# Attention on one core: value products for two head pairs at a time, and output products kept turned until the end of a batch

## The chip, the cores and the metric

The kernel runs on one core of one Trainium2 chip. The metric is the device time of one execution in microseconds (us), lower is better; a kernel's figure is the median of its runs. All data are float32 unless a row says bf16.

## The reference, cut to what matters

The program is one transformer-like block over x of shape (2, 1024, 128): a recurrent mixer, a feed-forward layer with one of 32 experts for each token, a multi-level (hierarchical) attention, and the same feed-forward layer again. The change is in the attention alone:

```python
qkv = x @ w_qkv.T                      # 16 heads of 64, x is layer-normed
q, k, v = split(qkv)
for level in range(...):               # level 0 and five coarser levels
    # coarser q, k are means of neighbours, coarser v are sums of neighbours
    A = exp(S - S.max(-1))             # S in blocks of 16, q of a block with k of the block before
    Ysum += A @ v;  Asum += A.sum(-1)
out = Ysum / (Asum + 1e-8)
out = out @ w_out.T + b_out            # summed over the 16 heads
x = x + out
```

## The kernel before, in words

The five engines run five instruction streams written by hand; semaphores alone join them. PE is TensorE, DVE VectorE, ACT ScalarE, POOL GpSimd, SP the engine that issues DMAs.

The attention (functions `b_pe`, `b_act`, `b_dve`, `b_pool_engine`, `b_sp`) works on 16 units: 2 batches of 1024 tokens times 8 pairs of heads (a pair is 128 columns). The tokens of the level 0 (1024) and the coarser ones (512 places) make 12 tiles of 128. FINE is the level 0, ROUGH the coarser levels. `b_pe` is a software pipeline of iterations n = 0 to 16; iteration n begins with the four products `project(n+1, ...)` (L1730), and then has, in this order: ROUGH scores of unit n (L1763, L1769), `project_last(n+1)` (L1737), `values(n+1)` (L1748: 12 products, the loaded operand a tile of tokens, the moving one the 128 columns of value weights), extra work of other layers (turning of x in iterations 2 and 3, routing of the next layer in 11 to 14), `weighted(n, FINE)` (L1800), `project_out(n-1)` (L1821: 8 products, the loaded operand 128 tokens of the unit's normalised output, the moving one 128 columns of output weights, so that tokens lie on partitions), `weighted(n, ROUGH)`, FINE scores of unit n+1, and `add_weights(n)` (L1810). Iteration 15 has no projections; 16 is the end.

What the other engines do in iteration n, in order:
- ACT: `copy_y(n-1)`, the four drains of `project` (L1916), the exponential of unit n FINE (L1931), the drains of `project_last` and of the values (L1920 to L1924), the exponential ROUGH (L1935).
- DVE: `soften(n, FINE)` (L2024, L2025, L2030: maximum, subtraction, transposition), `divide(n-1)` (L2034 to L2041: reciprocals of the sums), `soften(n, ROUGH)`, `gather_out(n-1, 0)` and `(n-1, 1)` (L2050, which waits for `project_out`), `coarsen(n+1)` (L2068, L2071).
- POOL: two multiplications that normalise unit n-1 (L2200), then `merge(n)` (L2137, five additions, after the exponential ROUGH of n), for which `add_weights(n)` waits. In between now and then: `add_bias` (L2165) and, for the second batch, the coarser sums and `pack(1)` (L2146).

The products of `project` with j = 0, 1, of `project_last`, `values` and `project_out` pass through two PSUM banks in turn; the list `filled` fixes the order, and `bank_free` waits for the reader two fillings back.

## Time and profile before

| | |
|---|---|
| median of 3 runs (lowest to highest) | 561.32 us (560.02 to 562.15) |
| the profiled execution | 560.87 us, span 559.1 us |
| mean granted PE clock | 0.969 |
| PE busy | 506.0 us, 91% |
| DVE busy | 425.8 us, 76% |
| ACT busy | 291.5 us, 52% |
| POOL busy | 250.6 us, 45% |

The attention takes the stretch from about 217 to 465 us. A float32 product shows as two MATMUL records and two weight loads. The rows quoted below are from stretches of this; their columns are start in us, length in us, engine, line, operation, and in brackets the idle time before with what ended it.

### The profile page before, as it was taken

To read this page: it belongs to the slowest core of one execution; us is meant where nothing else is said; L and a number is where in the kernel's file an instruction comes from. 1 tells how busy PE (TensorE), PEld (TensorE's weight loads), DVE (VectorE), ACT (ScalarE), POOL (GpSimd) and SP (SyncE) were. 2 spreads that over 40 slices of the span, in tenths; PEclk is the share of its full clock that TensorE was granted. 3 is DMA by queue.
4 is the path that set the end of the run, shared out by engine and by line. 5 is a ranking of instruction groups with operands and counts; after the bars stand their busy time and mean duration, and the time that the engine had idled before them with its cause. 6 is when DMAs were issued, how large, how long until landed. Compare 5 with 4: busy or idle time off the path is not lost.

```text
span 559.1 us, 16575 instructions
## 1 busy us (share of the span) xinstructions
PE 506.0 (91%) x6408; PEld 307.2 (55%) x6408; DVE 425.8 (76%) x979; ACT 291.5 (52%) x624; POOL 250.6 (45%) x294
## 2 busy tenths in 40 slices
PE   6989888888989998999999999999999967989991
PEld 3323232356544544777767777777777755644540
DVE  3396958988747766878899888899878988847762
ACT  3644254254458864666545555546644523448870
POOL 3556677655524454252244443233333335533542
PEclk9999899998999998999999999999999987899997
DMA  6899820000269962100000000000000000169964
GB/s 182 319 426 270 94 25 0 2 0 20 66 194 277 273 211 67 31 3 21 21 21 22 22 21 22 22 21 22 22 20 9 7 2 9 40 184 277 277 215 137
DMA packets 45325, 54.09 MB, mean 97 GB/s; under 512 B 10880, under 2 KB 36416, under 8 KB 44224
## 3 DMA queue, kind: packets, MB, share of 16 engines
q1 hardware_dynamic: 42688, 47.78, 29.6%
q0 software_dynamic: 2560, 5.26, 2.7%
q8 instruction: 51, 0.84, 0.6%
q14 instruction: 26, 0.21, 0.1%
HBM read 43.55 MB, written 9.48 MB: 95 GB/s over the span
## 4 chain that ended last, share of the span: by engine, by line
PE 63%; DVE 22%; issue 6%; DMA 3%; ACT 3%; POOL 2%; SPq 0%; DVEq 0%; POOLq 0%; ACTq 0%
PE psum L1249 9%; PE psum L1748 7%; PE psum L1730 7%; PE psum L1821 5%; PE psum L1800 5%; PE psum L1268 4%; PE psum L1769 3%; PE psum L1256 3%; DVE arena L761 3%; POOL sorted_x L1467 2%; DVE arena L755 2%; PE psum L277 2%; PE psum L278 2%; PE psum L1007 1%; DVE arena L2030 1%
## 5 line engine op out<-in xcount | busy, mean ns | idle before, releaser
L2200 POOL TENSOR_TENSOR arena<-arena 128x512 f32<-128x512 f32 x32 | 40.9, 1302 | 110.6 <-issue 103.9
L1495 POOL DMA_INDIRECT y_tok<-arena,to x48 | 46.6, 971 | 63.3 <-ACT arena L1318 62.1
L1916 ACT ACTIVATE arena<-psum 128x512 f32<-128x512 f32 x64 | 38.1, 597 | 47.4 <-PE psum L1730 44.4
L1730 PE MATMUL psum<-arena 128*128 128x512 f32 x128 | 59.2, 605 | 0.7 <-ACT arena L1899 0.7
L1249 PE MATMUL psum<-experts,arena 128*32 x96 | 50.2, 604 | 1.1 <-ACT arena L1308 1.1
L1249 PE MATMUL psum<-arena 128*32 128x512 f32 x288 | 50.9, 605 | 0.0
L661 POOL TENSOR_TENSOR arena<-arena 128x512 f32<-128x512 f32 x32 | 37.2, 1179 | 27.9 <-DVE arena L761 17.5
L1748 PE MATMUL psum<-arena 128*128 128x128 f32 x384 | 47.5, 278 | 0.8 <-ACT arena L1921 0.8
L1748 PEld LDWEIGHTS psum<-arena 128*128 128x128 f32 x384 | 45.2, 192 | 1.8 <-ACT arena L1921 1.8
L2137 POOL TENSOR_TENSOR arena<-arena 128x256 f32<-128x256 f32 (+4 forms) x75 | 33.6, 447 | 25.9 <-ACT arena L1935 18.9
L1730 PEld LDWEIGHTS psum<-arena 128*128 128x128 f32 x128 | 22.9, 189 | 35.4 <-issue 33.8
L1332 ACT ACTIVATE arena<-experts 128x768 f32 x48 | 40.1, 839 | 1.7 <-issue 1.4
L1467 POOL DMA_INDIRECT sorted_x<-arena,row x32 | 31.0, 969 | 20.3 <-DVE row L1099 11.8
L1391 DVE COPY arena<-psum 128x256 f32<-128x256 f32 x48 | 20.4, 425 | 25.4 <-PE psum L1256 25.0
L761 DVE TENSOR_TENSOR_SCAN arena<-psum,arena 128x512 f32<-128x512 f32 x32 | 39.1, 1269 | 0.0
L1800 PE MATMUL psum<-arena 64*64 64x64 f32 (+2 forms) x1728 | 36.9, 224 | 2.2 <-ACT arena L1931 1.4
L2050 DVE TENSOR_TENSOR x_tok<-x_tok,psum 128x512 f32<-128x512 f32 x30 | 20.6, 687 | 22.7 <-PE psum L1821 22.5
L1924 ACT ACTIVATE arena<-psum 128x512 f32<-128x512 f32 x48 | 28.7, 597 | 17.2 <-PE psum L1748 17.2
L1268 PEld LDWEIGHTS psum<-experts,arena 128*32 128x32 f32 x192 | 20.8, 110 | 30.2 <-issue 29.8
L1800 PEld LDWEIGHTS psum<-arena 64*64 64x64 f32 x1728 | 33.1, 138 | 6.3 <-ACT arena L1931 1.5
L1821 PE MATMUL psum<-arena 128*128 128x128 f32 x256 | 34.0, 286 | 2.7 <-POOL arena L2200 2.7
L755 DVE TENSOR_TENSOR arena<-arena,psum 128x512 f32<-128x512 f32 x32 | 19.9, 685 | 20.9 <-PE psum L293 20.7
(240 smaller groups left out, 1195.2 us busy)
## 6 DMA issues: line engine op xcount, KB each, us to landing
arena<-in_experts SPq DMA_DIRECT2D x48, 384.0 KB, 4.4
experts<-in_experts SPq DMA_DIRECT2D x8, 1536.0 KB, 17.3
arena<-sorted_x SPq DMA_DIRECT2D x48, 64.5 KB, 3.7
sorted_x<-zeros SPq DMA_DIRECT2D x2, 1536.0 KB, 14.3
arena<-in_w_qkv SPq DMA_DIRECT2D x16, 192.0 KB, 2.8
arena<-y_tok SPq DMA_DIRECT2D x8, 256.0 KB, 3.1
x_tok<-in_x SPq DMA_DIRECT2D x4, 256.0 KB, 4.6
arena<-in_w_out SPq DMA_DIRECT2D x16, 64.0 KB, 1.9
```

Of the source, the lines that this page charges most:

```text
L761: dve.tensor_tensor_scan(a_state[:, m, 1:CHUNK + 1], DECAYS[:, :], a_kv[m % HALF], a_state[:, m, 0:1], ALU.mult, ALU.add).then_inc(s["stat ...
L1249: mm = pe.matmul(bank[2 + s % 2][rows, :], f_gxt[s % 2][:, rows], weights, start=True, stop=True)
L1268: mm = pe.matmul(bank[6 + s % 2][SLOT_ROWS * j:SLOT_ROWS * j + SLOT_ROWS, 0:C], f_sht[s % 2][:, rows], weights, start=(half == 0), stop=(h ...
L1332: act.activation(f_w_act[s % 5], experts[:, bass.ds(expert_at[s], WROW)], ACT.Copy).then_inc(t["w_act"], 1)
L1467: pool.indirect_dma_start(out=sorted_x[k], out_offset=bass.IndirectOffsetOnAxis(ap=f_row[:, i:i + 1], axis=0), in_=row_of(k, i), in_offset ...
L1495: pool.indirect_dma_start(out=y_tok, out_offset=bass.IndirectOffsetOnAxis(ap=f_to[:, s:s + 1], axis=0), in_=f_gy[(s + 4) % 8], in_offset=N ...
L1730: pe.matmul(ring("in", n, j)[:, :], b_w[n % 2][:, which * P:which * P + P], x, start=True, stop=True)\
L1748: mm = pe.matmul(ring("in", n, 5 + i // 4)[:, i % 4 * P:i % 4 * P + P], x, b_w[n % 2][:, 2 * P:3 * P], start=True, stop=True)
L1800: mm = pe.matmul(place(Y[r][out]), b_v[n % 2][rows, i, out], e[rows, head, i - part.start, cols], start=(i == 0), stop=last_place(r, i, cols))
L1821: mm = pe.matmul(ring("out", n, i // 4)[:, i % 4 * C:i % 4 * C + C], b_yn[:, i * P:i * P + P], b_wo[n % 2], start=(n < LAST - 1 or n < LAS ...
L1916: act.activation((b_q, b_k)[which][:, part * CHUNK:part * CHUNK + CHUNK], src, ACT.Copy, scale=(D_B ** -0.5, 1.0)[which]).then_inc(h["drai ...
L2200: pool.tensor_tensor(b_yn[:, part], b_y[:, part], b_rec[:, part], ALU.mult).then_inc(h["normed"], 1)
```

## The change

Values: the loads of value weights are split off from those of q and k weights. `values(n)` runs for even n alone and makes the values of units n and n+1: the loaded token tile is the same, the moving operand is 256 columns. Iterations with odd n have this work, those with even n have none; the first stands ahead of iteration 0. Value drains on ACT are six in the one iteration (before: three in each). Outputs: for 13 units `project_out` loads the output weights and moves 512 tokens past them, twice, so that channels lie on partitions; the sums of a batch are kept so in `b_acc`. For the last unit of batch 0 and the last but one of batch 1 (`TURNED_BACK`), the sums are turned back by products of `b_acc` tiles with the identity into the bank, into which these units' outputs then go in the old way. The bias joins the first sum on DVE in place of POOL's `add_bias`. The normalised output replaces `b_y` in place. ACT packs only what of `b_odd` is used.

```diff
-            sp.dma_start(b_w[n % 2].rearrange("p (n c) -> p n c", c=P), w["w_qkv"][n % PAIRS]).then_inc(w_in[n % 2], 16)
+            sp.dma_start(b_w[n % 2].rearrange("p (n c) -> p n c", c=P), w["w_qkv"][n % PAIRS][:, 0:2]).then_inc(w_in[n % 2], 16)
+
+        def value_weights_in(sp, n):
+            two = w["w_qkv"][n % PAIRS:n % PAIRS + 2, :, 2:3].rearrange("u c n d -> c (n u) d")
+            sp.dma_start(b_wv.rearrange("p (u d) -> p u d", d=P), two).then_inc(wv_in, 16)
...
+        TURNED_BACK = (PAIRS - 1, LAST - 1)
...
             def values(n):
                 b = n // PAIRS
+                pe.wait_ge(wv_in, 16 * (n // 2) + 16)
                 for i in range(TILES_B):
-                    if i % 4 == 0:
-                        bank_free("in", n, 5 + i // 4)
+                    if i % 2 == 0:
+                        bank_free("in", n, 5 + i // 2)
...
-                    mm = pe.matmul(ring("in", n, 5 + i // 4)[:, i % 4 * P:i % 4 * P + P], x, b_w[n % 2][:, 2 * P:3 * P],
+                    mm = pe.matmul(ring("in", n, 5 + i // 2)[:, i % 2 * 2 * P:i % 2 * 2 * P + 2 * P], x, b_wv,
                                    start=True, stop=True)
...
+            def turn_sums(n, j):
+                pe.wait_ge(h["acc"], 2 * (n - 1) + j + 1)
+                for i in range(4):
+                    pe.matmul(ring("out", n, j)[:, i * C:i * C + C], b_acc[:, j * CHUNK + i * P:j * CHUNK + i * P + P], ident,
+                              start=(i == 0), stop=False)
+
             def project_out(n):
                 pe.wait_ge(wo_in[n % 2], 16 * (n // 2) + 16)
...
+                for j in range(2):
+                    out = ring("out", n, j)
+                    if n < LAST:
+                        bank_free("out", n, j)
+                    if n in TURNED_BACK:
+                        turn_sums(n, j)
+                    pe.wait_ge(h["normed"], 2 * n + j + 1)
+                    y = y_of(n)[:, j * CHUNK:j * CHUNK + CHUNK]
+                    if n in TURNED_BACK or n == LAST:
+                        for i in range(4):
+                            mm = pe.matmul(out[:, i * C:i * C + C], y[:, i * P:i * P + P], b_wo[n % 2], start=False,
+                                           stop=(n != LAST - 1 and i == 3))
+                    else:
+                        mm = pe.matmul(out, b_wo[n % 2], y, start=True, stop=True)
+                    mm.then_inc(h["o"], 1)
...
-                if new:
+                if new and n % 2 == 1:
                     values(n + 1)
...
             def gather_out(n, j):
-                dve.wait_ge(h["biased"], n // PAIRS + 1)
                 dve.wait_ge(h["o"], 2 * n + j + 1)
                 at = n // PAIRS * SEQ + j * CHUNK
-                part = slice(at, at + CHUNK)
-                dve.tensor_tensor(x_tok[:, part], x_tok[:, part], ring("out", n, j)[:, :], ALU.add)\
-                   .then_inc(h["acc"], 1)
+                part, acc = slice(at, at + CHUNK), b_acc[:, j * CHUNK:j * CHUNK + CHUNK]
+                if n % PAIRS == 0:
+                    dve.wait_ge(bias_in, 16)
+                    i = dve.tensor_scalar(acc, ring("out", n, j)[:, :], b_bias, None, ALU.add)
+                elif n % PAIRS == PAIRS - 1:
+                    i = dve.tensor_tensor(x_tok[:, part], x_tok[:, part], ring("out", n, j)[:, :], ALU.add)
+                else:
+                    i = dve.tensor_tensor(acc, acc, ring("out", n, j)[:, :], ALU.add)
+                i.then_inc(h["acc"], 1)
```

PE's stream before, from the start of iteration 3 to the output products of iteration 4 (left out: iteration 3's smaller products). Each iteration has its own `values`, L1748, between L1737 and L1800.

```order
L1730 MATMUL psum<-arena 128x512 x4
L1763 MATMUL psum<-attend_bf 128x256 x2
L1769 MATMUL psum<-arena 64x64 x16
L1737 MATMUL psum<-arena 128x128 x2
L1748 MATMUL psum<-arena 128x128 x12
L1800 MATMUL psum<-arena 64x64 x32
L1821 MATMUL psum<-arena 128x128 x8
```

The same engine now, in an iteration with even n. Nothing stands between L1757 (`project_last`) and L1821 (`weighted`), and L1856 is the output product.

```order
L1750 MATMUL psum<-arena 128x512 x4
L1784 MATMUL psum<-attend_bf 128x256 x2
L1790 MATMUL psum<-arena 64x64 x16
L1757 MATMUL psum<-arena 128x128 x2
L1821 MATMUL psum<-arena 64x64 x32
L1856 MATMUL psum<-arena 128x512 x2
```

And now in an iteration with odd n, where the twelve products L1769 have 256 columns.

```order
L1784 MATMUL psum<-attend_bf 128x256 x2
L1790 MATMUL psum<-arena 64x64 x16
L1757 MATMUL psum<-arena 128x128 x2
L1769 MATMUL psum<-arena 128x256 x12
L1821 MATMUL psum<-arena 64x64 x32
L1856 MATMUL psum<-arena 128x512 x2
```

So the value products of two iterations have moved together ahead of the FINE `weighted` of the odd one.

## Rows read from the trace of the kernel before

**Rows 1.** Stretch, length; busy PE, PEld, DVE, ACT, POOL; PE clock, DMA: iterations 0,2,4,7,10,12,14.

```profile
226.86:239.92 13.06, 12.56 (x255) 8.60 (x253) 9.58 (x35) 7.83 (x15) 5.68 (x8) 1.00 0.12 32
254.12:268.79 14.67, 14.67 (x276) 10.87 (x273) 12.16 (x22) 9.26 (x19) 4.69 (x7) 1.00 0.07 20
283.46:298.70 15.24, 14.62 (x272) 10.58 (x269) 14.23 (x28) 7.23 (x14) 5.97 (x10) 1.00 0.07 20
327.12:341.33 14.21, 14.21 (x273) 10.45 (x269) 12.29 (x22) 7.35 (x14) 4.70 (x7) 1.00 0.08 22
370.24:384.98 14.74, 14.58 (x273) 10.59 (x269) 13.65 (x32) 8.86 (x18) 5.90 (x8) 1.00 0.08 20
399.62:415.60 15.98, 15.73 (x285) 11.82 (x281) 12.28 (x23) 8.00 (x16) 4.69 (x7) 1.00 0.07 18
431.71:448.03 16.32, 15.01 (x274) 10.72 (x270) 15.73 (x28) 7.92 (x16) 5.91 (x9) 1.00 0.02 6
```

**Rows 2.** Timeline of PE in iteration 7.

```profile
327.12 3.70 PE L1730 MATMUL psum<-arena 128*128 128x512 f32 x8
...
331.59 0.71 PE L1737 MATMUL psum<-arena 128*128 128x128 f32 x4
332.14 2.90 PE L1748 MATMUL psum<-arena 128*128 128x128 f32 x24
334.97 1.16 PE L1800 MATMUL psum<-arena 64*64 64x64 f32 x64
336.06 2.05 PE L1821 MATMUL psum<-arena 128*128 128x128 f32 x16
338.04 1.08 PE L1800 MATMUL psum<-arena 64*64 64x64 f32 x44
```

**Rows 3.** Product lines by themselves: duration of one in ns, minimum/median/maximum.

```profile
L1748 PEld LDWEIGHTS psum<-arena x384: 186/192/192, 224.0 to 440.3; 128*128 128x128 f32 x192
L1748 PE MATMUL psum<-arena x384: 275/275/377, 224.1 to 440.4; 128*128 128x128 f32 x192
L1730 PE MATMUL psum<-arena x128: 592/592/697, 217.7 to 434.8; 128*128 128x512 f32 x128
```

**Rows 4.** Timeline of DVE in iteration 7 and the start of 8.

```profile
326.86 1.21 DVE L2024 TENSOR_REDUCE arena<-psum 128x16 f32<-128x1024 f32 x1
...
335.17 0.71 DVE L2030 STREAM_TRANSPOSE arena<-arena 128x512 f32<-128x512 f32 x1
...
340.94 1.21 DVE L2024 TENSOR_REDUCE arena<-psum 128x16 f32<-128x1024 f32 x1
```

**Rows 5.** Timeline of ACT in iteration 7: the exponentials and the last value drain.

```profile
331.35 1.05 ACT L1931 ACTIVATE arena<-arena 128x1024 f32<-128x1024 f32 x1
...
335.08 0.60 ACT L1924 ACTIVATE arena<-psum 128x512 f32<-128x512 f32 x1 [0.35 <-PE psum L1748]
335.92 0.81 ACT L1935 ACTIVATE arena<-arena 128x256 f32<-128x256 f32 x3 [0.24 <-DVE arena L2030]
```

**Rows 6.** Timeline of POOL: end of iteration 6, then iteration 7.

```profile
325.63 1.37 POOL L2146 COPY arena<-arena 128x128 f32<-128x128 f32 x6
333.23 2.54 POOL L2200 TENSOR_TENSOR arena<-arena 128x512 f32<-128x512 f32 x2 [6.23 <-issue]
336.81 2.48 POOL L2137 TENSOR_TENSOR arena<-arena 128x256 f32<-128x256 f32 x5 [1.04 <-ACT arena L1935]
```

**Rows 7.** Timeline of DVE: `soften` FINE of iterations 4 and 10.

```profile
285.00 1.21 DVE L2024 TENSOR_REDUCE arena<-psum 128x16 f32<-128x1024 f32 x1
...
371.27 1.22 DVE L2024 TENSOR_REDUCE arena<-psum 128x16 f32<-128x1024 f32 x1
```

**Rows 8.** Timelines of DVE and POOL around `add_bias` in iteration 3.

```profile
281.49 2.20 DVE L2068 TENSOR_TENSOR arena<-arena 128x128 f32<-128x128 f32 x1
...
281.16 2.38 POOL L2165 TENSOR_TENSOR x_tok<-x_tok,arena 128x1024 f32<-128x1024 f32 x1
```

**Rows 9.** Timeline of PE: output products of unit 15.

```profile
461.74 1.13 PE L1821 MATMUL psum<-arena 128*128 128x128 f32 x8 [2.30 <-POOL arena L2200]
```

More of the change, by code:

```diff
@@ L1545, in f_sp @@
             if k == 0:
-                for n in range(2):
-                    attention_weights_in(sp, n)
+                attention_weights_in(sp, 0)
+                value_weights_in(sp, 0)
+                attention_weights_in(sp, 1)
             else:
@@ L1562, in hybrid_block @@
         b_rstd = [b_rstd_all[:, CT * c:CT * c + CT] for c in range(STEPS)]
-        b_w = [carve(3 * P) for _ in range(2)]
+        b_w, b_wv = [carve(2 * P) for _ in range(2)], carve(2 * P)
         assert F_ROWS_AT <= B_EARLY_AT and used[0] <= F_LOOP_AT
@@ L1606, in hybrid_block @@
             if n + 1 < UNITS:
-                filled += [("in", n + 1, j) for j in range(IN) if j not in IN_Y]
+                filled += [("in", n + 1, j) for j in range(fills(n + 1)) if j not in IN_Y]
             filled += AMONG.get(n, [])
@@ L1685, in merged_columns, with y_of @@
                     (fine[64:128, :, 31:512:32], rough[64:128, :, 3, 48:64])]
+        def y_of(n):
+            return b_y if n < LAST else b_q[:, 0:SEQ]
         def last_place(r, i, cols):
@@ L1705, in bank_free @@
                     after(pe, h["y_out"], n - 1)
-                    after(pe, h["drained"], IN * (n - 1) + IN_Y[-1] + 1)
+                    after(pe, h["drained"], filled_by(n - 1) + IN_Y[-1] + 1 if n else 0)
                     return
@@ L1711, in bank_free @@
                     if kind == "in":
[L1712 removed]
+                        pe.wait_ge(h["drained"], filled_by(n) + j + 1)
                     elif kind == "turn":
@@ L1754, in scores @@
                 rough = part == ROUGH
-                pe.wait_ge(h["drained"], IN * n + (5 if rough else 4))
+                pe.wait_ge(h["drained"], filled_by(n) + (5 if rough else 4))
                 if rough:
@@ L1789, in weighted @@
                 pe.wait_ge(h["expd"], 2 * n + rough + 1)
-                pe.wait_ge(h["drained"], IN * n + (8 if rough else 7))
+                pe.wait_ge(h["drained"], filled_by(n // 2 * 2) + (11 if rough else 9))
                 if not rough:
@@ L1799, in weighted @@
                             for cols, place in places(r, i):
-                                mm = pe.matmul(place(Y[r][out]), b_v[n % 2][rows, i, out], e[rows, head, i - part.start, cols],
+                                mm = pe.matmul(place(Y[r][out]), values_of(n)[rows, i, out], e[rows, head, i - part.start, cols],
                                                start=(i == 0), stop=last_place(r, i, cols))
@@ L1902, in pack @@
             def pack(b):
-                for level in range(1, LEVELS + 1):
+                for level in range(3, LEVELS + 1):
                     act.wait_ge(h["pooled"], pooled_up_to(level, b))
@@ L1948, in copy_y @@
                 act.wait_ge(h["weighed"], 2 * n + 2)
-                after(act, h["normed"], 2 * n)
-                act.activation(b_y, psum[:, 4 * 512:6 * 512], ACT.Copy).then_inc(h["y_out"], 1)
+                if n < LAST:
+                    after(act, h["o"], 2 * n)
+                act.activation(y_of(n), psum[:, 4 * 512:6 * 512], ACT.Copy).then_inc(h["y_out"], 1)
             act.activation(b_warm, constant("half")[:, 0:1], ACT.Exp)
@@ L1957, in b_act @@
             pack(0)
-            for j in range(4, IN):
+            for j in range(4, fills(0)):
                 drain(0, j)
@@ L1974, in b_act @@
                 if new:
-                    for j in range(4, IN):
+                    for j in range(4, fills(n + 1)):
                         drain(n + 1, j)
@@ L2058, in coarsen @@
                 for which, a in enumerate((b_q, b_k)):
-                    dve.wait_ge(h["drained"], IN * n + 2 * which + 2)
+                    dve.wait_ge(h["drained"], filled_by(n) + 2 * which + 2)
                     if which == 0:
@@ L2078, in b_dve @@
                 dve.wait_ge(returned[j], 16 * (RUNS // 4 - 1))
-            for a in (b_odd, b_even):
-                chain(dve.memset(rough_columns(a)[:, :, 3, 0, 48:64], 0.0))
+            for a, deep in ((b_odd, 0), (b_even, 3)):
+                chain(dve.memset(rough_columns(a)[:, :, deep, 0, 48:64], 0.0))
             pool_first(0)
@@ L2198, in b_pool_engine @@
                     pool.wait_ge(h["divided"], 2 * n + j + 1)
-                    after(pool, h["o"], 2 * (n - 1) + j + 1)
-                    pool.tensor_tensor(b_yn[:, part], b_y[:, part], b_rec[:, part], ALU.mult).then_inc(h["normed"], 1)
+                    pool.tensor_tensor(y_of(n)[:, part], y_of(n)[:, part], b_rec[j], ALU.mult).then_inc(h["normed"], 1)
                 if n + 1 < LAST:
```

83 lines of the change are left out of this document (37 added, 46 removed).

## The prediction

> **What bounds the kernel now.** I read first the busy time by stretch, cut at the starts of the iterations [rows 1]. The reader is to see three things: the typical iteration (7) takes 14.21 us and PE is busy in all of it; DVE is busy 12.29 of the 14.21 us, so it is close behind; and iterations 4, 10 and 14 are longer while PE is not full in them (14.62 of 15.24, 14.58 of 14.74, 15.01 of 16.32), so there something else decides. The granted clock is 1.00 in all. Second, PE's timeline of iteration 7 [rows 2], from start to start: projections and ROUGH scores 4.47 us, `project_last` 0.55, values 2.83, `weighted` FINE 1.09, output products 1.98, and from 338.04 to the next start at 341.33 another 3.29. Third, the other engines in the same iteration [rows 4 to 6], for what PE would wait for if it came earlier.
>
> Call s the start of `soften` FINE on DVE. Here s is 326.86, 0.26 us before the iteration begins (327.12), and in iteration 8 340.94, 0.39 before. From s runs a chain through all engines: DVE's three pieces of work (soften FINE, divide, soften ROUGH) end at 335.17 + 0.71 = s + 9.02 [rows 4]; ACT's ROUGH exponential runs from 335.92 to 336.73, POOL's merge from 336.81 to 339.29 [rows 5, 6]; then PE's `add_weights` and the next iteration. How long this chain is when it alone decides is read from the iterations in which PE waited: iteration 10 has s = 371.27 and ends at 384.98, iteration 4 has s = 285.00 and ends at 298.70 [rows 1, 7]. That is 13.71 and 13.70 us from s to the end. So an iteration cannot be shorter than 13.7 us from its s, however little PE has to do, and with s 0.3 before its start that is 13.4 us. The typical iteration is only 0.8 us longer than that. This is the number on which the forecast rests.
>
> **The change part by part.**
>
> Value products, on PE. Of one pair of units, 48 products' records with 128 columns become 24 with 256. Start to start, a record of 128 columns takes (2.90 - 0.275) / 23 = 0.114 us, one of 512 (3.70 - 0.592) / 7 = 0.444 [rows 2, 3]: nearly in proportion to columns. One of 256 is in none of the rows; it lies between half of 0.444 = 0.222 and twice 0.114 = 0.228. I take 0.223, so 24 of them take 5.35 us where two sections took 5.66: 0.3 us less in a pair, 2.5 in all eight.
>
> Output products. 16 records of 128 columns (1.98 us) become 4 of 512; half the length of `project`'s eight is 1.82. So 0.16 less in each of 13 units, 2.1 in all. The sums turned back cost 16 records for each of two units: 16 x 0.114 = 1.8 us each. In iteration 8 they stand ahead of a wait and are mostly in its shadow (0.2 us on the path). After the output products of unit 14, PE waits 2.30 us for POOL until it can begin those of unit 15 at 461.74 [rows 9]; 1.8 us more fits in this. If that cover were gone it would cost 1.8 us.
>
> The moved values are what counts. An iteration with odd n now has 14.21 - 2.83 + 5.35 - 0.16 = 16.57 us of work on PE, 2.35 more than before; nothing on the other engines comes up to that. Seven of them (1 to 13): +16.45. In two of these (9 and 13) DVE starts late because of work for the next layer, and ACT's exponential, which stands ahead of the value drains, delays the second group of values by part of a drain; estimate 0.2 each, +0.4.
>
> An iteration with even n has only 14.21 - 2.83 - 0.16 = 11.22 us of work on PE. It does not take 11.22, for the chain needs 13.4. Followed in order, from the iteration's start: PE wants `weighted` FINE at 5.02; ACT's exponential of it ends at 332.40, or 5.28 after the start [rows 5], 0.4 us of waiting. It wants the output products at 6.6; POOL's first multiplication, 333.23 + 1.27, ends at 7.4 and the second at 8.65 [rows 6], 1.3 us of waiting in two parts, and the products end at 9.75. It wants `weighted` ROUGH then; the exponential ends at 9.61. It would be ready for `add_weights` at 12.1; merge ends at 12.17. With 0.2 for the release and 0.97 for the work: 13.4, the same from PE's side as from the chain. DVE cannot be further ahead at the start, for `gather_out` waits for the output products, which in the long iteration ahead stand behind the values; from their end DVE needs what it needs now, and s stays 0.3 before the start.
>
> The even iterations one by one, against their length now [rows 1]. Iteration 2: 14.67 to 13.4, -1.3. Iteration 4: 15.24 to 13.4, -1.85; 1.0 of this is `add_bias` that is gone, for DVE's addition next to it took 2.20 us instead of about 0.28 [rows 8]. Iterations 6 and 8: 14.21 to 13.6 (POOL's sums for the second batch lie late in the one, the sums turned back are in the other), -0.6 each. Iteration 10 is bound by the chain now and has its statistics on DVE ahead of s still: 0. Iteration 12 has 1.77 us of routing on PE, s at about -0.25: 15.98 to 13.7, -2.3. Iteration 14: bound by other engines now, 0. Iteration 0: the values of units 0 and 1 stand ahead of it, which moves its start by 2.5 us; after that its ROUGH scores, at 3.63 + 1.1, set off 2.2 of DVE, 0.85 of ACT, 2.5 of POOL and 1.2 of release and `add_weights`, 11.45 us in place of 13.06: +0.9. Together -5.75. Also `pack(1)` on POOL, 1.37 us, stands behind merge at the end of iteration 6 [rows 6], and PE waits for it before iteration 7; merge now ends only 1.2 us before the end: +0.4.
>
> Costs of nothing: the six value drains take 0.60 us each [rows 5] for every 0.89 us of filling, as now. `b_y` in place: `project_out(n-1)` stands ahead of `weighted(n, ROUGH)` on PE, and the copy waits for the latter anyway. The bias on DVE replaces an addition of the same size. The extra DMA on SP stands behind value products that are done two iterations before its data are wanted. ACT's shorter pack is in time in which ACT is idle (7.35 busy of 14.21 [rows 1]).
>
> Sum: 16.45 + 0.4 + 0.4 - 5.75 = +11.5 us. Against the profiled execution (560.87, of it 559.1 span; nothing ahead of the attention or behind it changes) this is 572.4. The profiled run lies 0.45 below the median of the three runs, 561.32; I put the forecast at 572.5.
>
> **The weight loads.** A value product of 128 columns has a load of 192 ns beside it, and the products follow each other every 114 ns [rows 3], so loads lie beside products and beside each other. If a section's pace were set by its loads, a product with 256 columns would take as long as one with 128.
>
> The Trainium skill, page "TensorE: Matmul & The Clock Gate", section "Back-to-back issue gap", says that in a stream of loads and products the spacing is set by both, with about 81 ns at 128 columns and 131 at 512. By that ratio of 1.6 the 512-column form would be far cheaper for each column; this trace has 0.444 to 0.114, a ratio of 3.9, for float32, so I go by the trace.
>
> **The rivals.**
> - The even iterations do shrink to PE's own work (faster). For this merge would have to end at 10 in place of 12.2, that is, s would have to lie 2.5 us before the start in place of 0.3; from 2.2 us on the loss begins to vanish. Then the even iterations save 3.0 (4.0 in iteration 4), 22 in all, against 16.9 + 0.4 for the odd ones and 1.8 for the sums turned back: about -3.5, 557 us. Against it stand iterations 4 and 10, where the chain held at 13.7 us twice. Chance 0.07.
> - The loads set the pace of the products (faster). The values of a pair then take 2.83 in place of 5.66. The odd iterations stay near 14.1, the even ones at 13.4: 16.45 falls to about -1, which gives 555 us. Against it: 114 ns under a load of 192. Chance 0.04.
> - No gain and no loss: the even iterations give back about as much as the odd ones take, for instance with the merge on POOL quicker in the gaps. It needs 1.6 us less in each even iteration. Chance 0.05.
> - The odd iterations also wait for ACT (slower still). Each group of two tiles is filled in 0.89 us and must be drained before the next but one; if the drain, now with a strided read, and the release take 0.3 us more than 0.60, six groups wait 0.15 each, 0.9 us in an iteration, and if the clock falls in the gaps of the even ones another 1 us each. Together +6 to +14 on the 11.5: about 580. Chance 0.12.
> - As worked out, with its own range of 568 to 577, as the chain is known to 0.3 us in eight iterations and the odd ones to 0.4: chance 0.72.
>
> **How the numbers follow.** The likeliest gives 572.5. To leave out no more than two in ten, the range takes in the lower part of the slower rival and some way towards no change: 564 to 580. Less than 0.5% (2.8 us) is about what a measurement of this kernel can't tell from no change. Faster by more: 0.07 x most of it and 0.04, 0.10. Within: 0.06. Slower: 0.84.
>
> **What would show it.** In the profile after, iterations with odd n should be 16.6 us with PE full, and those with even n 13.4 with PE busy about 11.2, waiting at `weighted` FINE for ACT, at the output product for POOL's multiplication, and at `add_weights` for POOL's merge. DVE, busy the same in both, should idle before `gather_out` for some 4 us in the odd ones and hardly in the even ones. Products of 256 columns should start every 0.22 us. The prediction is wrong if even iterations are below 13 us, if `values` takes less than 5.2 us, or if the waits stand in the odd ones.

## The result, and the profile after

The changed kernel takes 575.95 us (median of 4 runs, 573.62 to 576.79) against 561.63 us before (4 runs, 560.02 to 562.15): a ratio of 1.0247, 95% interval 1.0211 to 1.0282. The profiled execution is one of 575.73 us with a span of 573.9 us, 14.8 more than the span before, and a mean granted clock of 0.971 (before 0.969). PE is busy 509.0 us, 3.0 more than before, in a span 14.8 longer: its share has gone from 91% to 89%. The work has hardly changed, the waiting has.

I cut the trace at the starts of the iterations as before. Busy time by stretch of the changed kernel, iterations 0, 2, 4, 5, 7, 10, 12 and 14 (columns as in [rows 1]):

```profile
228.80:240.11 11.31, 9.83 (x229) 5.89 (x229) 8.03 (x25) 6.16 (x12) 4.59 (x7) 1.00 0.09 25
256.89:270.50 13.61, 12.40 (x240) 6.93 (x236) 12.85 (x22) 7.58 (x16) 4.70 (x7) 1.00 0.06 17
287.82:301.44 13.62, 12.05 (x237) 6.55 (x233) 12.86 (x22) 5.57 (x11) 5.69 (x9) 1.00 0.06 17
301.44:318.22 16.78, 16.78 (x261) 10.58 (x257) 11.78 (x22) 9.05 (x17) 6.38 (x12) 1.00 0.08 22
332.31:349.06 16.75, 16.75 (x256) 10.55 (x256) 11.49 (x21) 9.04 (x17) 4.51 (x7) 1.00 0.08 22
379.85:395.86 16.01, 13.32 (x237) 7.17 (x233) 14.11 (x32) 7.16 (x15) 5.81 (x8) 0.89 0.05 14
413.12:426.75 13.63, 13.26 (x248) 7.89 (x245) 12.87 (x25) 6.44 (x13) 4.70 (x7) 1.00 0.07 18
444.88:461.22 16.34, 12.41 (x238) 6.68 (x234) 15.79 (x28) 6.21 (x13) 5.75 (x9) 1.00 0.02 6
```

The reader is to see the alternation: with odd n (5, 7) 16.8 us and PE busy in all of it; with even n (2, 4, 12) 13.6 us, in which PE is not full and DVE is busy 12.9. Iteration 10 stands out with 16.01 us and a clock of 0.89.

PE's timeline in iteration 7, which answers to [rows 2]:

```profile
337.31 5.53 PE L1769 MATMUL psum<-arena 128*128 128x256 f32 x24
342.77 1.16 PE L1821 MATMUL psum<-arena 64*64 64x64 f32 x64
343.86 1.99 PE L1856 MATMUL psum<-arena 128*128 128x512 f32 x4
345.78 1.08 PE L1821 MATMUL psum<-arena 64*64 64x64 f32 x44
```

The values take 342.77 - 337.31 = 5.46 us (before 2.83), the output products 345.78 - 343.86 = 1.92 (before 1.98). And the same engine in iteration 4, an even one:

```profile
293.16 1.16 PE L1821 MATMUL psum<-arena 64*64 64x64 f32 x64
295.33 2.32 PE L1856 MATMUL psum<-arena 128*128 128x512 f32 x4 [1.01 <-POOL arena L2227]
297.65 1.08 PE L1821 MATMUL psum<-arena 64*64 64x64 f32 x44
...
300.42 1.09 PE L1831 MATMUL psum<-arena 64*64 64x512 f32 x8 [0.27 <-POOL arena L2177]
301.44 1.13 PE L1750 MATMUL psum<-arena 128*128 128x512 f32 x2
```

PE waits twice for POOL: 1.01 us for the normalisation (L2227), and again before `add_weights` (L1831) for the merge (L2177). The groups of the attention (212 to 480 us) say the same for all iterations; behind the second bar stand the idle times and what ended them:

```profile
L1769 PE MATMUL psum<-arena 128*128 128x256 f32 x192 | 44.8, 387 | 0.3 <-ACT arena L1953 0.2
L1821 PE MATMUL psum<-arena 64*64 64x64 f32 (+2 forms) x1728 | 37.8, 227 | 5.2 <-ACT arena L1964 2.9 <-ACT arena L1968 1.9
L1856 PE MATMUL psum<-arena 128*128 128x512 f32 x52 | 27.6, 638 | 7.2 <-POOL arena L2227 6.6
L1831 PE MATMUL psum<-arena 64*64 64x512 f32 x120 | 15.9, 602 | 1.5 <-POOL arena L2177 1.4
```

The value products (L1769), now in odd iterations alone, wait 0.3 us in all, in iterations 9 and 13.

**The books.** All figures are differences to before in us. The stretch ahead of the attention -0.77 (the first `project` starts at 216.91, before at 217.68; over the ten kernels of this text it starts at 216.9 to 220.7, so I take it for chance, which is not shown). The values of the second unit ahead of iteration 0, together with iteration 0: +0.96 (11.89 in place of 9.18, then 11.31 in place of 13.06). Odd iterations 1 to 13: +17.45. Even iterations 2 to 12: -4.47. Iteration 14: +0.02. From there to the second layer's scatter: -0.45. The second layer: +2.0, which is not the change's (below). Sum 14.7.

### The profile page after: what moved, and what is told of

It is laid out like the page before. It is cut to its first block, busy times and chain, and to the rows that moved or that the text cites. A ratio compares the mean times of both kernels' runs of the same rounds, so it can differ in the third digit from the quotient of the medians.

```text
span 573.9 us, 15923 instructions
## 1 busy us (share of the span) xinstructions
PE 509.0 (89%) x6092; PEld 281.6 (49%) x6092; DVE 425.5 (74%) x979; ACT 290.7 (51%) x618; POOL 243.1 (42%) x292
## 4 chain that ended last, share of the span: by engine, by line
PE 53%; DVE 28%; issue 7%; POOL 4%; DMA 3%; ACT 3%; SPq 0%; DVEq 0%; POOLq 0%; ACTq 0%
PE psum L1249 8%; PE psum L1769 7%; PE psum L1750 6%; PE psum L1268 4%; PE psum L1856 3%; PE psum L1256 3%; PE psum L1821 3%; DVE arena L2064 3%; DVE arena L2059 2%; DVE arena L761 2%; POOL sorted_x L1467 2%; DVE arena L2058 2%; PE psum L277 2%; DVE arena L755 2%; PE psum L278 2%
## 5 line engine op out<-in xcount | busy, mean ns | idle before, releaser
L2227 POOL TENSOR_TENSOR arena<-arena 128x512 f32<-128x512 f32 x32 | 37.6, 1195 | 112.1 <-DVE arena L2076 112.1
L1750 PE MATMUL psum<-arena 128*128 128x512 f32 x128 | 59.1, 605 | 1.0 <-ACT arena L1931 0.7
L2177 POOL TENSOR_TENSOR arena<-arena 128x256 f32<-128x256 f32 (+4 forms) x75 | 34.3, 458 | 45.5 <-ACT arena L1968 37.6
L661 POOL TENSOR_TENSOR arena<-arena 128x512 f32<-128x512 f32 x32 | 37.2, 1182 | 27.8 <-DVE arena L761 17.5
L1769 PE MATMUL psum<-arena 128*128 128x256 f32 x192 | 44.8, 387 | 0.3 <-ACT arena L1953 0.2
L1821 PEld LDWEIGHTS psum<-arena 64*64 64x64 f32 x1728 | 34.0, 140 | 19.7 <-ACT arena L1968 7.8
L1821 PE MATMUL psum<-arena 64*64 64x64 f32 (+2 forms) x1728 | 37.8, 227 | 5.2 <-ACT arena L1964 2.9
L1750 PEld LDWEIGHTS psum<-arena 128*128 128x128 f32 x128 | 23.0, 189 | 35.9 <-issue 34.4
L1769 PEld LDWEIGHTS psum<-arena 128*128 128x128 f32 x192 | 33.0, 189 | 9.8 <-ACT arena L1957 3.6
L755 DVE TENSOR_TENSOR arena<-arena,psum 128x512 f32<-128x512 f32 x32 | 19.8, 683 | 20.9 <-PE psum L293 20.7
L2090 DVE TENSOR_TENSOR arena<-arena,psum 128x512 f32<-128x512 f32 x22 | 14.8, 678 | 25.9 <-PE psum L1856 25.9
L1856 PE MATMUL psum<-arena 128*128 128x512 f32 x52 | 27.6, 638 | 7.2 <-POOL arena L2227 6.6
```

What stands on the lines that cost most here:

```text
L1750: pe.matmul(ring("in", n, j)[:, :], b_w[n % 2][:, which * P:which * P + P], x, start=True, stop=True)\
L1769: mm = pe.matmul(ring("in", n, 5 + i // 2)[:, i % 2 * 2 * P:i % 2 * 2 * P + 2 * P], x, b_wv, start=True, stop=True)
L1821: mm = pe.matmul(place(Y[r][out]), values_of(n)[rows, i, out], e[rows, head, i - part.start, cols], start=(i == 0), stop=last_place(r, i, ...
L1856: mm = pe.matmul(out, b_wo[n % 2], y, start=True, stop=True)
L2227: pool.tensor_tensor(y_of(n)[:, part], y_of(n)[:, part], b_rec[j], ALU.mult).then_inc(h["normed"], 1)
```

## Lengths of the iterations in all kernels

Call s, as in the prediction, the start of `soften` FINE on DVE; the chain is the time from s to the end of the iteration, and the lead is how far s lies ahead of the iteration's start.

Each experiment below has one thing to be read from its trace before its whole time: how long the iterations are. Lengths in us, from the starts of the `project` products in PE's timeline of each profiled execution; "0 to 13" is the sum of iterations 0 to 13, "ahead" the time from the first `project` to iteration 0.

| kernel | ahead | 1 | 2 | 4 | 5 | 7 | 8 | 9 | 10 | 11 | 12 | 0 to 13 |
|---|---|---|---|---|---|---|---|---|---|---|---|---|
| before | 9.18 | 14.20 | 14.67 | 15.24 | 14.21 | 14.21 | 14.21 | 14.70 | 14.74 | 14.64 | 15.98 | 204.85 |
| changed | 11.89 | 16.78 | 13.61 | 13.62 | 16.78 | 16.75 | 13.62 | 17.17 | 16.01 | 17.26 | 13.63 | 216.08 |
| values per unit | 9.18 | 14.15 | 14.60 | 14.15 | 14.15 | 14.15 | 16.00 | 15.01 | 14.46 | 14.58 | 15.91 | 204.95 |
| paired values only | 11.89 | 16.84 | 13.57 | 15.49 | 16.85 | 16.81 | 13.57 | 16.84 | 15.96 | 17.32 | 13.70 | 217.88 |
| no values | 11.90 | 12.93 | 13.00 | 12.98 | 12.98 | 12.68 | 13.48 | 14.90 | 15.15 | 13.70 | 13.13 | 189.02 |
| statistics later | 11.89 | 16.78 | 13.63 | 13.59 | 16.79 | 16.75 | 13.61 | 17.18 | 13.68 | 17.26 | 13.74 | 213.84 |
| values spread | 11.89 | 14.09 | 14.86 | 14.64 | 14.10 | 14.10 | 16.18 | 14.96 | 15.49 | 14.53 | 16.03 | 207.66 |
| spread, statistics later | 11.89 | 14.09 | 14.86 | 14.64 | 14.09 | 14.10 | 16.18 | 14.96 | 14.64 | 15.54 | 16.03 | 207.83 |
| merge cut short | 11.89 | 16.78 | 13.06 | 12.99 | 16.78 | 16.79 | 13.47 | 17.17 | 14.52 | 17.26 | 13.13 | 211.79 |
| wait alone | 9.18 | 14.20 | 14.67 | 15.45 | 14.21 | 14.21 | 14.21 | 15.02 | 14.96 | 14.65 | 15.97 | 205.46 |

Iterations repeat to a few hundredths from kernel to kernel where nothing in them is changed (1, 9 and 11 of the changed kernel, of the one with late statistics and of the one with the merge cut short). The rest of a program does not: from iteration 14's start to the end of the span it is 127.4 us before and 128.1 to 134.3 in the others, though behind the attention the instructions are the same. So small effects are read from iterations.

## The experiments

**The values unit by unit again, all other edits kept.**

```diff
-            return 5 + (VALUES if n % 2 == 0 else 0)
+            return 8
...
-                if new and n % 2 == 1:
+                if new:
                     values(n + 1)
```

> The kernel after, with only the value products put back to one unit in each iteration (12 products of 128 columns); transposed outputs, sums turned back, bias on DVE and y in place stay. My theory (the alternation of long and short iterations is the loss): the whole loss goes. Typical iterations 14.05 us (14.21 less 0.16 for the output products), iteration 4 about 14.1 as the bias addition on POOL is gone, so about 558 to 561 us, 1 to 3 below the kernel before. Rival (the other edits cost something: sums turned back, wider transfers, output products that wait for the normalised half): 564 or more. Rival (the wide product itself is slow): also 558 to 561, so that one is told apart by the second kernel of this call and by its rows.

Measured: 564.07 us, before on the same chip 565.43, ratio 0.9981 (0.9950 to 1.0013). The alternation is gone, and with it the whole loss. The expected totals were reckoned from a kernel before of 561; on this chip it takes 565.43, so the difference counts, 1.4 us less where 1 to 3 were expected, and the interval does not tell it from none. Two iterations of this kernel, 7 and 8, by stretch:

```profile
328.30:342.45 14.15, 14.15 (x260) 9.27 (x257) 12.49 (x22) 7.36 (x14) 4.62 (x7) 1.00 0.07 21
342.45:358.45 16.00, 16.00 (x289) 12.24 (x285) 12.30 (x24) 7.36 (x14) 4.50 (x7) 1.00 0.07 19
```

In 7, PE is full at 14.15, 0.06 less than before: that is all that the output products' new form is worth in an iteration. In 8 the sums are turned back, and where PE is full they cost 16.00 - 14.21 = 1.79 us. In the changed kernel iteration 8 is an even one with 13.62, as long as iteration 2 without them: there they lie wholly in the wait for POOL. Iteration 4 falls from 15.24 to 14.15, which is `add_bias` gone [rows 8]. So the other edits come to nothing together: iterations 0 to 13 take 204.95 us against 204.85.

**Before, with paired values alone.** The old output products, `add_bias` on POOL and the separate `b_yn` stay; the values, their weight loads, buffers and drains are those of the change (and `b_zt` lies in `b_s`, for room).

```diff
-                if new:
+                if new and n % 2 == 1:
                     values(n + 1)
```

> The kernel before, with only the value products of two units at a time (and the buffers that this needs); output products, bias on POOL and the rest stay. My theory: nearly the whole loss is here: odd iterations 16.8 to 16.9 us, even ones 13.6 to 13.8, total 575 to 579, a little above the kernel after because the output products keep 1.98 us and the bias stays on POOL. Rival (other edits carry half of it): 568 or less.

Measured: 584.45 us, ratio 1.0323 (1.0273 to 1.0373), more than expected. By iterations: 217.88 - 204.85 = 13.0 in 0 to 13, and 2.7 ahead of them, 15.7 together, near the 13 to 17 us that 575 to 579 meant; the excess lies outside the attention, where this trace is 3.0 us longer ahead of it and 6.4 us from iteration 14 on. Compared with the changed kernel the one large difference is iteration 4 (15.49 against 13.62), `add_bias` again. Its stretches of an odd and an even iteration:

```profile
307.14:323.99 16.85, 16.85 (x273) 11.77 (x269) 11.72 (x22) 9.05 (x17) 6.41 (x12) 1.00 0.08 21
354.84:368.41 13.57, 12.15 (x249) 7.89 (x245) 12.74 (x26) 5.57 (x11) 4.69 (x7) 1.00 0.06 18
```

So the paired values alone make the loss, and the other edits give 1.8 us of it back (217.88 against 216.08), nearly all of it by the bias in iteration 4.

**No values behind the first pair.** All iterations lack the value products, their drains and loads behind the first two units (later units use the first pair's values), so every iteration is as empty as an even one.

```diff
-            return 5 + (VALUES if n % 2 == 0 else 0)
+            return 5 + (VALUES if n == 0 else 0)
...
-                if new and n % 2 == 1:
-                    values(n + 1)
```

> The kernel after, with the value products, their drains and their weight loads left out behind the first pair (later units use the first values, so the output is not the reference's). All iterations then have only 11.2 us of work on PE. My theory (a chain through DVE, ACT and POOL sets a floor of 13.6 us): every typical iteration is 13.6 us, odd ones too, total about 576 - 7 x 3.2 = 553. Rival (PE's own work sets the pace and the short iterations are long for a reason that belongs to the values): iterations of 11.2 to 12, total near 530.

Measured: 554.32 us in two runs, ratio 0.9804 (0.9762 to 0.9845), near the 553 expected. Typical iterations take 12.98 us, neither the 13.6 of the one theory nor the 11.2 to 12 of the other. From s to the iteration's end it is 13.94 to 13.96 in iterations 2 to 5, the same as in the even iterations of the changed kernel (13.94 to 13.96 in 2, 4, 8 and 12). What differs is the start: s lies 0.96 before the iteration's start in a row of short iterations, and 0.33 behind a long one. So the prediction's chain holds, and the length is chain minus lead; that the lead grows where all iterations are short I had not expected. Iterations 9 and 10 (14.90 and 15.15) are longer because s comes late there and, in 10, the clock falls too. A typical iteration by stretch:

```profile
281.88:294.86 12.98, 12.04 (x237) 6.54 (x233) 12.22 (x22) 5.56 (x11) 5.69 (x9) 1.00 0.06 18
```

Even without any value work PE could not have been filled: this is 1.2 us below the typical iteration before, for 2.83 us of work taken out.

**The second half's statistics of the next layer one iteration later.** In iteration 10 the start of `soften` on DVE stands behind these statistics, which run there from 379.52 on. What follows from them on POOL moves one iteration on as well.

```diff
                 if n >= 1:
                     divide(n - 1)
+                if n == PAIRS + 3:
+                    front_shift(dve, 1, 1)
...
                 if n == PAIRS + 1:
-                    sums_of(PAIRS - 1, 1)
                     front_shift(dve, 1, 0)
                 if n == PAIRS + 2:
-                    front_shift(dve, 1, 1)
+                    sums_of(PAIRS - 1, 1)
```

> The kernel after, with the statistics of the second half of batch 0 on DVE moved from the end of iteration 9 to the end of iteration 10 (and what follows from them on POOL and DVE one iteration on). My theory: iteration 10 has a late start of soften (1.1 us), so PE stands idle longer there, its granted clock falls to half for 3.4 us, and it takes 16.0 us; moved behind, iteration 10 takes 13.6 us, iteration 11 at most 0.4 more than 17.3, total 2.0 to 2.5 us below the kernel after. Rival (the clock fall comes from something else, or the late start only moves): below 1 us.

First the rows of the changed kernel: PE in iteration 10, and two stretches of 1 us in it.

```profile
385.87 1.16 PE L1821 MATMUL psum<-arena 64*64 64x64 f32 x64 [0.72 <-ACT arena L1964]
388.82 3.00 PE L1856 MATMUL psum<-arena 128*128 128x512 f32 x4 [1.79 <-POOL arena L2227]
391.75 1.77 PE L1821 MATMUL psum<-arena 64*64 64x64 f32 x44
...
390.30:391.30 1.00, 1.00 (x2) 0.02 (x1) 0.50 (x1) 1.00 (x4) 0.14 (x1) 0.52 0.00 0
391.30:392.30 1.00, 1.00 (x21) 0.55 (x24) 0.44 (x1) 1.00 (x4) 0.92 (x2) 0.50 0.09 16
```

PE has waited 0.72 and then 1.79 us; behind that the granted clock is 0.50, 1.2 GHz in place of 2.4, and the output products take 3.00 us, against 2.32 in iteration 4. The waits go ahead of the fall, but they do not settle it. In the kernel with the merge cut short (described below) iteration 10 has the same two waits, and its clock stays at 1.00, with a length of 14.52:

```profile
386.84 1.16 PE L1821 MATMUL psum<-arena 64*64 64x64 f32 x64 [0.72 <-ACT arena L1964]
389.79 2.33 PE L1856 MATMUL psum<-arena 128*128 128x512 f32 x4 [1.79 <-POOL arena L2227]
```

With the statistics later:

```profile
380.21:393.89 13.68, 12.03 (x236) 6.54 (x233) 12.88 (x26) 6.98 (x15) 4.70 (x7) 1.00 0.06 17
```

13.68 in place of 16.01, a clock of 1.00, and iteration 11 as before at 17.26: 2.3 us for moving one piece of DVE work. The kernel measured 578.72 us (ratio 1.0242, 1.0205 to 1.0279, before at 565.43), 13.3 us above before on its chip, against 14.3 for the changed one on another; the whole time is too coarse to show the 2.0 to 2.5 us expected of it.

**The values of a pair spread over two iterations.** The loaded tile and the 256 columns stay. Six tiles stand behind the FINE `weighted` of the even iteration, where the even unit's buffer is free, six in the old place of the odd one. ACT's third drain of the even iteration stands behind the exponential ROUGH.

```diff
-            return 5 + (VALUES if n % 2 == 0 else 0)
+            return 11 if n == 0 else 8 if n < LAST else 5
...
                 if now:
                     weighted(n, FINE)
+                if n % 2 == 0 and n + 1 < LAST:
+                    values(n + 1)
```

> The changed kernel with everything it has (values of two head pairs for each loaded tile, 256 columns moved; outputs moved past loaded output weights), but the same twelve tiles of a pair of units are spread over two iterations: six tiles behind the FINE weighted of the even iteration, six in the old place of the odd one. Theory (the loss is only that work was taken from iterations that cannot become short and put into ones that PE fills): PE's work is 11.22 + 2.7 = 13.9 us in each iteration and the floor of 13.6 is below it, so every typical iteration takes 13.9 to 14.2 us, none 16.8, and the kernel ends 11 to 17 us before the changed one, at a ratio to before of 0.990 to 1.000. Rival (products of 256 columns with their strided drains, or the third value buffer, cost something by themselves): odd and even iterations at 14.5 or more and a ratio to before of 1.008 or more.

Measured: 571.38 us, before 564.01 on the same chip, ratio 1.0129 (1.0095 to 1.0163): 1.3% slower, a miss, and a ratio that the rival had named. Half of it was right: no iteration is 16.8 any more, and the odd ones are 14.10. Three things were wrong. The even ones take 14.64 in place of 13.9 to 14.2; stretches of 5 and 6, and PE in iteration 4:

```profile
302.45:316.55 14.10, 14.10 (x249) 8.56 (x245) 12.66 (x22) 7.36 (x14) 5.87 (x9) 1.00 0.09 26
316.55:331.18 14.63, 14.44 (x248) 8.54 (x244) 12.29 (x22) 7.50 (x17) 6.68 (x16) 1.00 0.06 16
...
294.23 2.95 PE L1778 MATMUL psum<-arena 128*128 128x256 f32 x12
297.02 2.21 PE L1866 MATMUL psum<-arena 128*128 128x512 f32 x4
299.16 1.08 PE L1831 MATMUL psum<-arena 64*64 64x64 f32 x44
```

The output products (L1866) take 2.14 us from start to start in place of 1.92, as the second of them wants the bank that ACT's late drain empties, and ahead of its `weighted` PE waits some 0.3 us for ACT's exponential, which before lay under the values; the place of the values in this iteration is mine, not a property of paired values. Nor had I counted the sums turned back: in iteration 8, where PE is now full, they make 16.18 us, 1.5 more than in iterations 4 and 6. And I had not counted the first pair: its second unit costs 2.71 us ahead of iteration 0 (11.89 against 9.18), which comes back only if an iteration at the end gets shorter, and iteration 14 cannot, being bound by DVE (busy 15.79 of 16.34). Those 2.7 and the 2.8 in iterations 0 to 13 are 5.5 of the 7.4 us; the rest is not placed. Against the changed kernel iterations 0 to 13 are 216.08 - 207.66 = 8.4 us shorter with the same products. So in the odd iterations the long products are no dearer by themselves (14.10, 0.05 less than with values per unit), and most of the changed kernel's loss is their distribution. But pairing gains nothing in this order either: against the kernel with values per unit, iterations 0 to 13 are 2.7 us longer (207.66 against 204.95), and the stretch ahead of them another 2.7.

**The spread kernel with the late statistics too.** The edits of the last two runs together.

> The spread kernel and, on top, the second half's statistics of the next layer one iteration later (as in the run in which this took 2.3 us from iteration 10). Theory: the spread kernel's iterations 9 and 10 are the ones in which PE still waits for the chain that starts late on DVE; with the statistics later iteration 10 loses 0.3 to 1 us and iteration 11 gains less than 0.3, so this is the fastest of the kernels, ratio to before 0.988 to 0.999. Rival (iteration 10 is filled by PE's own work once the values are spread, so that a late start on DVE is hidden): the same time as the spread kernel within 0.3 us.

Measured: 570.87 us, ratio 1.0138 (1.0100 to 1.0176): no change against the spread one, and a miss against the 0.988 to 0.999 expected. Iteration 10 loses 0.85 (15.49 to 14.64), as expected, and iteration 11 takes 1.01 more (14.53 to 15.54), which was not expected: now DVE starts late there, 1.05 us behind the iteration's start, and PE is full enough in both that the work comes out in one or the other. In the changed kernel with late statistics iteration 11 has the values of two units, which fill PE, and s was only 0.42 us late there, so the delay was hidden.

**The merge cut to its first addition.** The sums lack four of the five parts.

```diff
-        MERGES = LEVELS
+        MERGES = 1
...
-                for j, (whole, some) in enumerate(merged_columns(b_e[n % 2])):
+                for j, (whole, some) in enumerate(merged_columns(b_e[n % 2])[0:1]):
```

> The changed kernel with only the first of POOL's five additions of the merge (the sums of weights lack four of five coarser levels' parts, so the output is not the reference's). The merge takes 0.74 us instead of 2.4 to 2.7. The prediction named one chain, which goes over DVE's ROUGH softening, ACT's ROUGH exponential and this merge, 13.6 us for an even iteration. If this chain alone held the even iterations, they would fall to 11.9 and the kernel by some 11 us. The theory now: PE's own way, which waits 1.0 us at the output product for POOL's normalisation and then has products up to the FINE scores without a gap, ends only 0.3 us before the merge, so even iterations fall from 13.62 to 13.3 and the kernel by 2 to 3 us; odd iterations stay at 16.8.

Measured: 577.97 us in the one run against 564.01 before on its chip, 14.0 more, where the changed kernel had 14.3: the whole time shows nothing. But iterations 0 to 13 take 4.3 us less, 1.5 of it in iteration 10, whose clock did not fall. An even iteration falls from 13.62 to 12.99, 0.63 and not the 1.7 that one chain alone would give, twice the 0.3 that I expected. Odd ones stay. PE and POOL in iteration 6:

```profile
327.85 2.33 PE L1856 MATMUL psum<-arena 128*128 128x512 f32 x4 [0.90 <-POOL arena L2227]
330.16 1.08 PE L1821 MATMUL psum<-arena 64*64 64x64 f32 x44
...
332.47 1.04 PE L1831 MATMUL psum<-arena 64*64 64x512 f32 x8
...
330.19 0.74 POOL L2177 TENSOR_TENSOR arena<-arena 128x256 f32<-128x256 f32 x1 [1.25 <-ACT arena L1968]
```

The merge is over at 330.93, and PE comes to `add_weights` only at 332.47, with no wait: from the normalisation on it has products without a gap. From s to the end it is 13.45. So there are two chains, one over the merge (13.95) and one over `divide`, POOL's normalisation and the output products (13.45), and taking the first away brings 0.5 and the lead that goes with it.

**The new wait on DVE alone.** The change also puts the turned sums of weights `b_zt` into `b_s`, the buffer that the softening's transposition is reading; for this `divide` waits for that transposition's end. This experiment is the kernel before with that alone.

```diff
-        b_zt, b_rec, b_yn = carve(SEQ), carve(SEQ), carve(SEQ)
+        b_zt, b_rec, b_yn = b_s[:, 0:SEQ], carve(SEQ), carve(SEQ)
...
                 dve.wait_ge(h["summed"], n + 1)
+                dve.wait_ge(h["turned"], 2 * min(n + 1, LAST) + 1)
                 dve.transpose(b_zt, psum[:, 6 * 512:8 * 512]).then_inc(h["z_out"], 1)
```

> The kernel before with one side effect of the change alone: the turned sums of weights (b_zt) lie in the softening's buffer b_s, so that DVE waits for the end of its own FINE transposition before it turns the sums. In the changed kernel this second transposition starts 1.35 us after the first, in the kernel before 1.17 us. Theory (this wait is what makes the chain from s to the iteration's end 13.95 us in the changed kernel instead of 13.70): with it, the iterations of before that the chain decides (4, 9 and 10) take 13.95 us from s, 0.2 to 0.25 longer each, and those that PE fills (5, 7, 8: 14.21 us) do not change; the whole ends within 1 us, ratio 0.998 to 1.003. Rival (the 0.25 comes from the output products' new form or the gaps on PE): the chain stays at 13.70 here.

Measured: 565.82 us against 564.79, ratio 1.0022 (1.0000 to 1.0044). The chain from s is 13.92, 13.93 and 13.93 in iterations 4, 9 and 10 (before 13.70, 13.70, 13.71), and iterations 5, 7 and 8 stay at 14.21. Two transpositions of DVE in iteration 4, first before, then in this kernel:

```profile
287.50 1.25 DVE L2030 STREAM_TRANSPOSE arena<-arena 128x1024 f32<-128x1024 f32 x1
288.67 1.21 DVE L2034 STREAM_TRANSPOSE arena<-psum 128x1024 f32<-128x1024 f32 x1
...
289.75 1.25 DVE L2030 STREAM_TRANSPOSE arena<-arena 128x1024 f32<-128x1024 f32 x1
291.10 1.25 DVE L2035 STREAM_TRANSPOSE arena<-psum 128x1024 f32<-128x1024 f32 x1
```

1.17 us from start to start without the wait, 1.35 with it: the second no longer begins 0.08 us before the first one's end but 0.10 behind it. It also takes 1.25 us itself in place of 1.21. Together that is 0.22, the whole of what this chain grew by, and 0.22 of the 0.25 in the changed kernel. The edit moves the buffer as well as adding the wait; that the later start is the wait's is read from its lying behind the end, and what made the second transposition 0.04 longer is not shown.

## Why the prediction was right, point by point

**The chain that bounds even iterations** was the number on which the forecast rested: 13.4 us forecast, 13.61 to 13.63 measured (2, 4, 8, 12). The lead of s was put at 0.3 and is 0.33. The chain was taken from before at 13.7 and is 13.95, because a side effect of the change, the wait of `divide` for DVE's own transposition, was not in my list of parts; the run with the wait alone shows 0.22 of it. The prediction had PE's own way end level with the merge (12.1 and 12.17); the run with the merge cut short shows it 0.5 us shorter. Iterations 2 and 4 gave 1.06 and 1.62 where 1.3 and 1.85 were forecast.

**The odd iterations**: forecast +2.35 each and 0.2 more in two, 16.85 together; measured 17.45. The step for the pace was right, (5.53 - 0.378) / 23 = 0.224 us from record to record against the 0.223 taken, but I multiplied it by 24 for the whole section and set this against 2.83, which has the handing over to the next products in it (24 x 0.114 is 2.74). The section is 5.46, not 5.35. The output products give 0.06, not 0.16: the half of eight products that I used halves also what the start and the end of a section add. The 0.2 for ACT in iterations 9 and 13 was no addition: the values take 5.86 and 5.83 us there in place of 5.46, but the same wait stood there before (3.20 and 3.11 in place of 2.83).

**Iteration 0 and the values ahead of it**: +0.9 forecast, +0.96 measured. **`pack(1)`** behind the merge: iteration 6 at 14.09 is 0.12 shorter than before, against 0.2 (0.6 less the 0.4) forecast. **Iteration 12**: -2.35, forecast -2.3. **Iteration 14**: 0.02, forecast 0. **Sums turned back**: forecast 0.2 on the path in iteration 8 and 0 at the end; measured 0 and 0. For the end, PE's rows behind unit 14's products, where [rows 9] had a wait of 2.30:

```profile
473.18 1.06 PE L1853 MATMUL psum<-arena 128*128 128x128 f32 x8
474.56 1.13 PE L1853 MATMUL psum<-arena 128*128 128x128 f32 x8 [0.32 <-POOL arena L2227]
```

The 1.8 us went into that wait. Where PE is full, as in the run with values per unit, they cost the 1.79 us named for a cover that is gone.

**Iteration 10** is the one term that failed. I put it at 0, since the chain bounds it before and after, and it took 1.27 us more. The chain gives 0.25 of this and a start of s 0.1 later gives 0.1; the other 0.9 is the clock, which fell to half behind PE's waits. I had the falling clock among the rivals for all even iterations; it came in one, the one in which PE waits longest, and with the same waits it can stay away (the merge cut short). Whether it falls I could not have told from these rows.

**What is not the change's.** 2.0 of the 14.8 us lie in the second layer. Last of POOL's scatters and SP's fetches of their rows, before and in the changed kernel:

```profile
494.64 0.96 POOL L1467 DMA_INDIRECT sorted_x<-arena,row  x1 [0.30 <-issue]
497.22 1.75 SPq L1523 DMA_DIRECT2D arena<-sorted_x  x4
...
507.37 0.96 POOL L1467 DMA_INDIRECT sorted_x<-arena,row  x1 [0.30 <-issue]
511.87 1.28 SPq L1527 DMA_DIRECT2D arena<-sorted_x  x3
```

From the last scatter's issue to the first fetch it is 2.58 us before and 4.50 in the changed kernel. No instruction there is changed, and in the eight experiments the same step takes 2.8 to 4.3 us; from the first fetch to the end it is 61.9 and 62.0 us. So the forecast of +11.5 stands against +12.7 that the traces give to the change (14.7 less 2.0), and of the distance from 572.5 to 575.95 (3.5 us, of which 0.3 lies between span and median) 1.2 us are the attention's and 2.0 this variation. The 1.2 are small by luck: the iterations were put too low by 2.5 us (odd ones 0.6, even ones 1.8, of which 1.3 is iteration 10, the rest 0.1), and the stretches ahead of and behind them came out 1.2 shorter, which no term foresaw. I can't say why the fetches began later in that execution; it was not tried.

**The signs.** The waits stand where they were named. DVE's idle time before `gather_out` is 4.44 us in iteration 5 and 0.38 in iteration 4, as foreseen. Two signs were off. PE's busy time in even iterations is 12.05 us in iteration 4, not 11.2, as short waits do not all show as idle time: `weighted` FINE begins 5.34 us after the start in place of 5.02 with no idle time noted, and the output products count as busy for 2.32 us in place of 1.99. And DVE is not busy the same in both, 12.9 us in even iterations and 11.8 or less in the typical odd ones (1, 3, 5, 7), because `soften` of an odd iteration starts about 1 us before it, while the even one still runs.

**The rivals.** Even iterations at PE's own 11.2: excluded by the even ones at 13.6, and by the run without values, in which none of 1 to 13 is below 12.68. (The sum of this rival is -2.9 us by its own terms, 22 against 19.1, not -3.5.) No gain and no loss: it needed 1.6 us less in each even iteration; they came out 0.2 above the forecast. Loads that set the pace: excluded by 0.224 us for 256 columns; their weight loads take 189 ns at the median beside products of 378. The Trainium skill, page "TensorE: Matmul & The Clock Gate", section "Back-to-back issue gap", gives spacings of about 81 ns at 128 columns and 131 at 512; here, in float32, the three widths stand at 0.114, 0.224 and 0.444 us, in proportion to columns, so moving more columns past a load saves next to nothing. Odd iterations that wait for ACT: their PE is full, and a value drain takes 599 ns at the mean against 597 before, so the strided read costs nothing that shows.

## What to carry to other kernels

Where iterations of a pipeline alternate, each has its own floor: work can be taken out of an iteration only down to the longest chain through the other engines, while all that is added to a full one counts. Before work is gathered into every second iteration, take the chain's length from an iteration in which the bottleneck engine already waited, subtract its lead, and compare it with the gap that would come about; here 0.6 us could be had where 2.8 was taken out, and 2.6 was paid. And ask first whether the gathered form does less work at all: here 24 long products took 5.46 us where two sections of 24 short ones had taken 5.66. And list the waits that a change adds for room in memory: they are part of the chain too.

## What the runs showed of the hardware that was not expected

A wait of DVE for its own last instruction costs: 0.18 us from start to start at two transpositions of 1.25 us, 0.22 on the chain. The Trainium skill, page "VectorE: DVE Perf Modes", section "The DRAIN you can't avoid", has eight copies taking 13.88 us whether each or only the last has a semaphore behind it, by which the added wait would be free; for this pair of transpositions the measurement says otherwise.

The granted clock fell to 0.50 in iteration 10, where PE had waited 0.72 and then 1.79 us, and stayed at 1.00 in iteration 4 with its waits of 1.01 and 0.27. But in iteration 10 of the kernel with the merge cut short PE waited the same 0.72 and 1.79 us, and in iteration 9 of the one without values 0.66 and 1.79, and the clock stayed at 1.00. So a fall has to be reckoned with behind waits of this size, and what decides it these traces do not show. Iteration 10 of the changed kernel with its DVE work moved had a clock of 1.00 and was 2.33 us shorter, of which about 1.4 is the earlier s and 0.9 the clock.
